# The norm roots' Newton steps and the exponentials' biases from VectorE to GpSimd, with a new order of work in the layers

## The chip, the cores and the metric

One core of a Trainium2 chip runs the whole program; the seven other cores are idle. The metric is the device time of one execution in microseconds (us). The kernel before takes 3483.93 us, the median of three runs (3475.66 to 3485.28).

## What is computed

Eight sequences ("images" below) of 512 tokens with 128 features go through a linear attention of Taylor features with a norm on either side, then through six layers, each of a local attention (16 heads of 64, windows of 32 tokens) and a gated feed-forward block, and through a last norm. All of it is float32. The change lies in the six layers:

```python
def attn_layer(x, Wqkv, qs, ksc, Wo):
    q, k, v = split(x @ Wqkv)               # 16 heads of 64
    q = l2norm(q) * qs
    k = l2norm(k) * ksc
    q = q * cos * scale + rotate_half(q) * sin * scale
    k = k * cos * inv + rotate_half(k) * sin * inv
    sim = q @ k2.T * 8                      # window and the one before it
    sim = where(mask, -big, sim)
    return (softmax(sim) @ v2) @ Wo

def ffn_layer(x, g, bln, W1, b1, W2, b2):
    xn = (x - mean(x)) / sqrt(var(x) + 1e-5) * g + bln
    a, gate = split(xn @ W1 + b1)
    return a * gelu(gate) @ W2 + b2

for i in range(6):
    x = attn_layer(shift_tokens(x), ...) + x
    x = ffn_layer(shift_tokens(x), ...) + x
```

## The kernel before

The program has no loop on the chip. `order()` lays every step of the whole run on one line by a time: a step of slot n stands at n plus its entry in the table `PLACE`. Each of the five engine programs walks this line and issues the instructions of its own steps in that order, with explicit waits on semaphores. So the table alone decides what is queued behind what, on each engine and on the DMA queue of SyncE (SP). An engine that waits holds up all that follows on it.

The layers have 48 units (one image in one layer). A unit has 8 slots of one head pair each and 4 rounds of two slots each; round m has the head pairs of slots 2m and 2m+1. The steps of one head pair lie many slots apart, so that a round mixes work of several pairs. The steps that matter here:

- `PJ` (TensorE): projection of Q and K of a head pair, three matmuls (`PS<-LXH,LH`, `PS<-LXL,LH`, `PS<-LXH,LL`) into one PSUM bank. `VP` is the same for V (`PS<-LH,LXH` and two more), `VC` its copy to `VV` on ScalarE.
- `PQ` (ScalarE, L1221): squares `SX`. `SS` (TensorE, `PS<-SX,C`): their sums over each head, 8 slots' halves to one PSUM tile.
- `PT` (VectorE, L938): the rotary products `TPB`, four per round; when it ends, the bank of its `PJ` is free. Projections, Wo and the feed-forward matmuls (`group`) share a ring of three banks, so that a `PJ` waits for the `PT` or copy that emptied the bank three groups earlier.
- `TS` (SP): swaps the halves of each pair through a DMA into `TR`. `AD` (GpSimd, L1350) adds them: final Q and K.
- `NM1`, `NM2`: norm roots for four slots at once, so twice in a unit. `NM1` takes the sums from PSUM (VectorE, L946) and does logarithm and exponential on ScalarE (L1024, L1026); `NM2` is one Newton step in three VectorE instructions on `NV` (L951, L953, L955, 128x128 each). `RW` (SP) writes the roots to DRAM, `RB` (SP, L518) reads them back as rows over 64 partitions, `PR` (GpSimd, L1332) multiplies K by them. `RQ` transposes them for the queries.
- `S1` (TensorE, mask `PS<-maskb,identb` and then `PS<-K,Q`): the scores of a round in banks 0 and 1. It waits for `PR` and for the exponentials of the round before, `S3`.
- `MX` (VectorE): the row maximum (L962), and then the exponential's bias `BQ`, minus the maximum times the query's root (L967, 128x16).
- `S3` (ScalarE, L1245): 16 exponentials with `BQ` as their bias, in four parts.
- `SU` (VectorE, L973, L975): sum and reciprocal. `NP` (GpSimd, L1358) scales by it. `TT` (VectorE, L981, L984): transposes. `PX`, `PY` (SP): move parts of them into `PP`.
- `PV` (TensorE, `PS<-PP,VV`): the product with V, in two halves (`PV` 0 and 1), and `PVn` (ScalarE) its copy.
- `WO` (TensorE, `PS<-AOT,LO`): Wo, once in a unit, and its addition to `X` on VectorE (L991, L992). Then the norm `F1`, `F2`, `F2n`, `F3` and the block `F4`, `F5`.

By what they hold besides the common steps, the four rounds of a unit are called here the plain round, the Wo round (`WO`, `NM1`, `NM2`), the norm round (`F1`, `F2`, `F2n`, `F3`) and the block round (`F4` and `F5` of that image, `NM1`, `NM2`).

Of the kernel before, what the change touches and what calls it, by code (L numbers as in the profile page):

```python
# [10 lines left out]
ALU = mybir.AluOpType  # L11
# [4 lines left out]
F1 = 341  # L16
# [10 lines left out]


PLACE = {
# [13 lines left out]
}  # L43

CONST = {}
# [261 lines left out]
def build(nc, xin, cst, awq, awk, awv, awo, wqkv, wo, w1, w2, vec, out):  # L307
    o = order()
    no = o.no
    with ExitStack() as ctx:  # L310
# [138 lines left out]
        def sync_program(e):  # L449
# [10 lines left out]
            for st, key in o.line:  # L460
# [40 lines left out]
                elif st == "RW":  # L501
                    q, = key
                    if q > 1:
                        for n in (4 * q - 6, 4 * q - 5):
                            on.wait_ge(f"rb_in{n % 2}", 32 * (n // 2) + 32)
                    on.wait_ge("nm_dve", 4 * q + 4)
                    for c in range(4):
                        e.dma_start(rootd[q % 2, :, 128 * c:128 * c + 128], NV[32 * c:32 * c + 16, 2, :]).then_inc(sem[f"rr_in{q % 2}"], 16)
                elif st == "RB":
# [29 lines left out]
        def tensor_program(e):  # L539
# [9 lines left out]
            for st, key in o.line:  # L549
# [135 lines left out]
                elif st == "SS":  # L685
                    i, = key
                    if i % 8 == 0 and i:
                        on.wait_ge("nm_dve", 4 * (i // 8) - 3)
                    on.wait_ge("pj_act", i + 1)
                    sel = cn("tsel")[:, 32 * (i % 8):32 * (i % 8) + 32]  # L690
                    for c in range(4):
# [35 lines left out]
                    p.then_inc(sem["s1_pe"], 1)  # L727
                elif st == "RQ":
                    q, = key
                    on.wait_ge("nm_dve", 4 * q + 4)  # L730
                    free(on, st, key)
                    e.transpose(bk(st, key)[:, 0:128], NV[:, 2, :], ident).then_inc(sem["rq_pe"], 1)
                elif st == "PV":
# [66 lines left out]
        def vector_program(e):  # L800
# [35 lines left out]
            for st, key in o.line:  # L836
# [104 lines left out]
                elif st == "NM1":  # L941
                    q, = key
                    if q:
                        on.wait_ge("nm_dve", 4 * q)
                    on.wait_ge("ss_pe", 8 * q + 8)
                    e.tensor_scalar(NV[:, 0, :], nb[:, 0:128], 1e-24, None, ALU.max).then_inc(sem["nm_dve"], 1)  # L946
                elif st == "NM2":
                    q, = key
                    v, u, x = NV[:, 0, :], NV[:, 1, :], NV[:, 2, :]
                    on.wait_ge("nm_act", 2 * q + 2)  # L950
                    e.tensor_tensor(u, v, x, ALU.mult).then_inc(sem["nm_dve"], 1)  # L951
                    on.wait_ge("nm_dve", 4 * q + 2)
                    e.scalar_tensor_tensor(u, u, -0.5, x, ALU.mult, ALU.mult).then_inc(sem["nm_dve"], 1)  # L953
                    on.wait_ge("nm_dve", 4 * q + 3)
                    e.scalar_tensor_tensor(x, u, 1.5, x, ALU.add, ALU.mult).then_inc(sem["nm_dve"], 1)  # L955
                elif st == "MX":
                    m, = key
                    g = PS[:, 0:2, :].rearrange("p s (g k) -> p (s g) k", k=64)
                    on.wait_ge("s1_pe", m + 1)
                    if m:  # L960
                        on.wait_ge("s1_dve", 2 * m)
                    e.tensor_reduce(MX[:, :], g, AX_X, ALU.max).then_inc(sem["s1_dve"], 1)  # L962
                    on.wait_ge("s1_dve", 2 * m + 1)
                    if m > 1:
                        on.wait_ge("s3_act", 4 * m - 4)
                    on.wait_ge("rq_act", m // 2 + 1)
                    e.scalar_tensor_tensor(BQ[m % 2][:, :], MX[:, :], -1.0, rq(m), ALU.mult, ALU.mult).then_inc(sem["s1_dve"], 1)  # L967
                elif st == "SU":
                    m, = key
                    if m > 1:  # L970
# [47 lines left out]
        def scalar_program(e):  # L1018
# [20 lines left out]
            for st, key in o.line:  # L1039
# [182 lines left out]
                elif st == "NM1":  # L1222
                    q, = key
                    if q:
                        on.wait_ge(f"rr_in{(q - 1) % 2}", 64 * ((q - 1) // 2) + 64)
                        on.wait_ge("rq_pe", q)
                    on.wait_ge("nm_dve", 4 * q + 1)
                    ln_exp(NV[:, 1, :], NV[:, 0, :], NV[:, 2, :], -0.5, "nm_act", q + 1)
                elif st == "VC":
                    j, = key  # L1230
# [5 lines left out]
                elif st == "S3":  # L1236
# [2 lines left out]
                    if m > 1:  # L1239
                        on.wait_ge("tt_dve", 2 * m - 2)  # L1240
                    on.wait_ge("rq_act", m // 2 + 1)
                    on.wait_ge("s1_dve", 2 * m + 2)
                    for g in range(4 * h, 4 * h + 4):
                        at = 64 * (g - 8 * s)
                        p = e.activation(SC[m % 2][:, g, :, :].rearrange("p x k -> p (x k)"), bank[s][:, at:at + 64], ACT.Exp,  # L1245
# [38 lines left out]
        def gpsimd_program(e):  # L1284
# [4 lines left out]
            for st, key in o.line:  # L1289
# [27 lines left out]
                elif st == "WL":  # L1317
# [6 lines left out]
                        hi, lo, src = LH[:, 256 * c:256 * c + 256], LL[:, 256 * c:256 * c + 256], WS[:, i % 3, :]  # L1324
                    on.wait_ge("wc_act", i + 1)
                    e.tensor_tensor(lo, src, hi.bitcast(F32), ALU.subtract).then_inc(sem["wc_pool"], 1)
                elif st == "PR":
                    n, = key
                    dst = K[:, n % 8, :]
                    on.wait_ge("ad_pool", 2 * n + 2)  # L1330
                    on.wait_ge(f"rb_in{n % 2}", 32 * (n // 2) + 32)
                    e.tensor_tensor(dst, dst, RB[n % 2][:, :], ALU.mult).then_inc(sem["pr_pool"], 1)  # L1332
                elif st == "XSl":
                    u, = key
                    b = u % NB
                    xh, xl = LX[u % 2]
                    on.wait_ge("xs_act", u + 1)
                    e.tensor_tensor(xl[:, :], X[:, b, 0:L], xh[:, :].bitcast(F32), ALU.subtract).then_inc(sem["xs_pool"], 1)
                elif st == "F3l":
                    u, = key  # L1340
                    on.wait_ge("xc_act", u + 1)
                    e.tensor_tensor(XCL[:, :], H[2][:, :], XCH[:, :].bitcast(F32), ALU.subtract).then_inc(sem["xc_pool"], 1)
                elif st == "AD":
                    i, = key
                    n, w = i // 2, i % 2
                    if n > 7:
                        on.wait_ge("s1_pe", n // 2 - 3)
                    on.wait_ge("pj_dve", i + 1)
                    on.wait_ge(f"t3_in{n % 2}", 32 * (n // 2) + 32)
                    e.tensor_tensor((Q, K)[w][:, n % 8, :], TPB[:, n % 3, w, :], TR[n % 2][:, w, :], ALU.add).then_inc(sem["ad_pool"], 1)  # L1350
                elif st == "NP":
                    m, = key
                    on.wait_ge("su_dve", 2 * m + 2)
                    if m == 0:
                        for z in PP:
                            e.memset(z[:, :, :, :], 0.0).then_inc(sem["zero_pool"], 1)
                    sc = SC[m % 2][:, :, :, :].rearrange("p g x k -> p g (x k)")
                    e.tensor_tensor(sc, sc, RC[m % 2][:, :].rearrange("p (g o) -> p g o", o=1).broadcast_to([128, 16, 64]),  # L1358
                                    ALU.mult).then_inc(sem["np_pool"], 1)
# [64 lines left out]
```

## Time and profile before

| what | value |
|---|---|
| median of three runs | 3483.93 us (3475.66 to 3485.28) |
| profiled execution, its own time | 3475.88 us |
| its span, first to last instruction | 3474.1 us |
| TensorE (PE) | 3179.2 us, 92% |
| weight loads (PEld), beside PE | 1975.5 us, 57% |
| VectorE (DVE) | 2763.6 us, 80% |
| ScalarE (ACT) | 2536.5 us, 73% |
| GpSimd (POOL) | 2044.8 us, 59% |

The profiled execution is one execution of the program. Its busy time of an engine is the time in which at least one of its instructions runs by the trace; the end of a matmul is modelled, so PE's share is an upper bound. Idle time is put down to what came last of all that the instruction waited for. The layers' first maximum starts at 580.1 us and the last at 3402.0 us, with 192 rounds; what is ahead is the linear attention, which the change leaves as it is.

### The profile page before, as it was taken

How to read it: one execution, taken by the hardware profiler on the slowest of the kernel's cores; microseconds unless marked ns; L12 is line 12 of the kernel's file. 1: busy time of each engine (PE TensorE's matmuls, PEld its weight loads, DVE VectorE, ACT ScalarE, POOL GpSimd, SP SyncE). 2: the span in 40 equal slices, each digit the busy share in tenths (PEclk: the TensorE clock that was granted, in tenths of full speed). 3: DMA queues.
4: the chain of work that ended last, by engine and by line, in shares of the span. 5: the costliest groups of instructions: out<-in, count | busy, mean ns of one | idle time of the engine just before them, and what ended most of it. 6: DMA issues, size and time to landing. Idle time of an engine off the chain costs nothing.

```text
span 3474.1 us, 125058 instructions
## 1 busy us (share of the span) xinstructions
PE 3179.2 (92%) x52744; PEld 1975.5 (57%) x52744; DVE 2763.6 (80%) x3420; ACT 2536.5 (73%) x5866; POOL 2044.8 (59%) x1559
## 2 busy tenths in 40 slices
PE   7999997899999999999999899999999999999986
PEld 3444434566666566656666566666666665655553
DVE  3656657888888888888888888888888888888883
ACT  4666664778777777768787878787777777787784
POOL 0000006767677666767677777677767676766661
PEclk9999998999999999999999999999999999999998
DMA  3223324444444444444444444444444444434431
GB/s 110 77 75 80 80 57 135 140 142 136 145 149 145 135 134 145 144 140 137 140 136 148 138 151 138 140 141 152 146 142 137 134 146 139 143 127 145 137 130 31
DMA packets 271821, 447.01 MB, mean 129 GB/s; under 512 B 84254, under 2 KB 122396, under 8 KB 271132
## 3 DMA queue, kind: packets, MB, share of 16 engines
q1 hardware_dynamic: 244944, 422.50, 37.3%
q10 hardware_dynamic: 26316, 16.52, 1.7%
q8 instruction: 415, 6.80, 0.8%
q14 instruction: 146, 1.20, 0.1%
HBM read 124.21 MB, written 7.34 MB: 38 GB/s over the span
## 4 chain that ended last, share of the span: by engine, by line
PE 47%; DVE 24%; ACT 13%; issue 7%; SPq 3%; DMA 2%; POOL 2%; DVEq 0%; ACTq 0%; POOLq 0%
PE PS L542 47%; DVE TPB L938 8%; ACT SC L1245 8%; DVE SM L973 2%; DVE MX L962 2%; ACT SX L1221 2%; DMA RB<-root_scratch 2%; DVE NV L953 2%; DVE NV L951 1%; DVE PP L981 1%; POOL K L1332 1%; DVE H L1006 1%; SPq L477 1%; DVE NV L955 1%; ACT H L1024 1%
## 5 line engine op out<-in xcount | busy, mean ns | idle before, releaser
L938 DVE SCALAR_TENSOR_TENSOR TPB<-PS,VEC,C 128x1024 f32<-128x1024 f32 x768 | 959.1, 1269 | 98.7 <-ACT SX L1221 91.2
L1245 ACT ACTIVATE SC<-PS,BQ,RQ 128x64 f32<-128x64 f32 x3072 | 977.7, 437 | 40.0 <-DVE BQ L967 39.8
L1221 ACT ACTIVATE SX<-PS 128x512 f32<-128x512 f32 x768 | 468.6, 638 | 355.0 <-PE PS L542 347.9
L1332 POOL TENSOR_TENSOR K<-K,RB 128x512 f32<-128x512 f32 x384 | 496.2, 1292 | 286.8 <-DMA RB<-root_scratch 273.4
L1358 POOL TENSOR_TENSOR SC<-SC,RC 128x1024 f32<-128x1024 f32 x192 | 366.1, 1907 | 409.3 <-DVE RC L975 409.3
L542 PE MATMUL PS<-LXH,LH 128*128 128x512 f32 x768 | 379.2, 494 | 153.3 <-DVE TPB L938 145.9
L1350 POOL TENSOR_TENSOR K<-TPB,TR 128x512 f32<-128x512 f32 x384 | 499.2, 1300 | 0.0
L1350 POOL TENSOR_TENSOR Q<-TPB,TR 128x512 f32<-128x512 f32 x384 | 497.6, 1296 | 0.0
L542 PEld LDWEIGHTS PS<-PP,VV 64*64 64x64 f32 x12288 | 279.8, 136 | 149.7 <-issue 146.2
L542 PE MATMUL PS<-PP,VV 64*64 64x96 f32 (+1 forms) x12288 | 352.6, 250 | 4.3 <-DMA PP<-PX 2.0
L542 PE MATMUL PS<-AOT,LO 128*128 128x512 f32 x768 | 342.4, 599 | 0.0
L973 DVE TENSOR_REDUCE SM<-SC 128x16 f32<-128x1024 f32 x192 | 234.0, 1219 | 125.3 <-ACT SC L1245 123.8
L542 PE MATMUL PS<-K,Q 64*32 64x64 f32 (+1 forms) x24576 | 307.8, 225 | 26.8 <-issue 15.0
L542 PEld LDWEIGHTS PS<-LXH,LH 128*128 128x128 f32 x768 | 145.5, 189 | 313.1 <-DVE TPB L938 183.9
L542 PEld LDWEIGHTS PS<-K,Q 64*32 64x32 f32 x24576 | 293.0, 106 | 49.1 <-issue 19.9
L542 PE MATMUL PS<-LXH,LL 128*128 128x512 f32 x768 | 307.3, 400 | 0.0
L542 PE MATMUL PS<-LXL,LH 128*128 128x512 f32 x768 | 306.1, 399 | 0.0
L1235 ACT COPY VV<-PS 128x512 f32<-128x512 f32 x384 | 239.1, 623 | 89.2 <-PE PS L542 86.2
L542 PE MATMUL PS<-SX,C 128*32 128x128 f32 x6144 | 254.8, 283 | 2.2 <-issue 1.3
L542 PEld LDWEIGHTS PS<-AOT,LO 128*128 128x128 f32 x768 | 142.0, 190 | 170.4 <-issue 170.2
L962 DVE TENSOR_REDUCE MX<-PS 128x16 f32<-128x1024 f32 x192 | 233.2, 1214 | 5.6 <-PE PS L542 5.1
L1298 POOL TENSOR_TENSOR XR<-XR,T 128x512 f32<-128x512 f32 x8 | 10.2, 1276 | 365.6 <-DVE T L908 365.6
(166 smaller groups left out, 5862.8 us busy)
## 6 DMA issues: line engine op xcount, KB each, us to landing
TR<-TPB SPq DMA_DIRECT2D x768, 256.0 KB, 2.7
RB<-root_scratch SPq DMA_DIRECT2D x768, 128.0 KB, 3.0
PP<-PX SPq DMA_DIRECT2D x576, 64.0 KB
PP<-PP SPq DMA_DIRECT2D x384, 64.0 KB, 2.4
WS<-in_wqkv ACTq DMA_DIRECT2D x72, 128.0 KB, 2.5
PP<-PX SPq DMA_DIRECT2D x192, 48.0 KB
QA<-TH SPq DMA_DIRECT2D x128, 64.0 KB, 2.1
QA<-TL SPq DMA_DIRECT2D x128, 64.0 KB, 2.1
```

The costliest lines, as they stand in the source:

```text
L477: e.dma_start((QA, KA)[n][c::4, g % 6, :].bitcast(F32), (TH, TL)[low][rows, n, half, :].bitcast(F32)).then_inc(sem[f"qk_in{g % 2}"], 16)
L542: return e.matmul(dst, lhsT, rhs, start=start, stop=stop, **kw)
L938: e.scalar_tensor_tensor(TPB[:, n % 3:4 + n % 2:3 + n % 2 - n % 3, w, :], g, VEC[:, l, 9 + w:10 + w], C[:, at:at + 1024].rearrange("p (o c ...
L953: e.scalar_tensor_tensor(u, u, -0.5, x, ALU.mult, ALU.mult).then_inc(sem["nm_dve"], 1)
L962: e.tensor_reduce(MX[:, :], g, AX_X, ALU.max).then_inc(sem["s1_dve"], 1)
L973: e.tensor_reduce(SM[:, :], SC[m % 2][:, :, :, :].rearrange("p g x k -> p g (x k)"), AX_X, ALU.add).then_inc(sem["su_dve"], 1)
L1221: e.activation(SX[i % 3][:, :], bk("PJ", key)[:, :], ACT.Square).then_inc(sem["pj_act"], 1)
L1235: e.copy(VV[:, c, 512 * hf:512 * hf + 512], bk("VP", key)[:, :]).then_inc(sem["vp_act"], 1)
L1245: p = e.activation(SC[m % 2][:, g, :, :].rearrange("p x k -> p (x k)"), bank[s][:, at:at + 64], ACT.Exp, bias=BQ[m % 2][:, g:g + 1], scale ...
L1332: e.tensor_tensor(dst, dst, RB[n % 2][:, :], ALU.mult).then_inc(sem["pr_pool"], 1)
L1350: e.tensor_tensor((Q, K)[w][:, n % 8, :], TPB[:, n % 3, w, :], TR[n % 2][:, w, :], ALU.add).then_inc(sem["ad_pool"], 1)
L1358: e.tensor_tensor(sc, sc, RC[m % 2][:, :].rearrange("p (g o) -> p g o", o=1).broadcast_to([128, 16, 64]), ALU.mult).then_inc(sem["np_pool" ...
```

## The change

The Newton step `NM2` goes from three VectorE instructions to four on GpSimd. `MX` stays on VectorE as a maximum that is written negated, and its product with the query's root goes to GpSimd. The semaphores are split accordingly (`nm_pool`, `bq_pool`). All entries of `PLACE` for the layers' steps are new; those of the linear attention are the same.

```diff
 PLACE = {
-    "LS": 221.000, "LB": -1.200, "LO": -0.800, "S1": -0.074, "MX": 0.116, "S3": (0.544, 0.762, 0.998, 1.143),
+    "LS": 221.000, "LB": -1.200, "LO": -0.800, "S1": -0.240, "MX": -0.000, "S3": (0.424, 0.992, 0.802, 0.799),
...
                 elif st == "RW":
-                    on.wait_ge("nm_dve", 4 * q + 4)
+                    on.wait_ge("nm_pool", 4 * q + 4)
...
                 elif st == "NM1":
                     q, = key
                     if q:
-                        on.wait_ge("nm_dve", 4 * q)
+                        on.wait_ge("nm_pool", 4 * q)
                     on.wait_ge("ss_pe", 8 * q + 8)
                     e.tensor_scalar(NV[:, 0, :], nb[:, 0:128], 1e-24, None, ALU.max).then_inc(sem["nm_dve"], 1)
-                elif st == "NM2":
-                    q, = key
-                    v, u, x = NV[:, 0, :], NV[:, 1, :], NV[:, 2, :]
-                    on.wait_ge("nm_act", 2 * q + 2)
-                    e.tensor_tensor(u, v, x, ALU.mult).then_inc(sem["nm_dve"], 1)
-                    on.wait_ge("nm_dve", 4 * q + 2)
-                    e.scalar_tensor_tensor(u, u, -0.5, x, ALU.mult, ALU.mult).then_inc(sem["nm_dve"], 1)
-                    on.wait_ge("nm_dve", 4 * q + 3)
-                    e.scalar_tensor_tensor(x, u, 1.5, x, ALU.add, ALU.mult).then_inc(sem["nm_dve"], 1)
                 elif st == "MX":
                     m, = key
                     g = PS[:, 0:2, :].rearrange("p s (g k) -> p (s g) k", k=64)
                     on.wait_ge("s1_pe", m + 1)
                     if m:
-                        on.wait_ge("s1_dve", 2 * m)
-                    e.tensor_reduce(MX[:, :], g, AX_X, ALU.max).then_inc(sem["s1_dve"], 1)
-                    on.wait_ge("s1_dve", 2 * m + 1)
-                    if m > 1:
-                        on.wait_ge("s3_act", 4 * m - 4)
-                    on.wait_ge("rq_act", m // 2 + 1)
-                    e.scalar_tensor_tensor(BQ[m % 2][:, :], MX[:, :], -1.0, rq(m), ALU.mult, ALU.mult).then_inc(sem["s1_dve"], 1)
+                        on.wait_ge("bq_pool", m)
+                    e.tensor_reduce(MX[:, :], g, AX_X, ALU.max, negate=True).then_inc(sem["s1_dve"], 1)
...
                 elif st == "S3":
...
-                    on.wait_ge("s1_dve", 2 * m + 2)
+                    on.wait_ge("bq_pool", m + 1)
...
+                elif st == "MX":
+                    m, = key
+                    on.wait_ge("s1_dve", m + 1)
+                    if m > 1:
+                        on.wait_ge("s3_act", 4 * m - 4)
+                    on.wait_ge("rq_act", m // 2 + 1)
+                    e.tensor_tensor(BQ[m % 2][:, :], MX[:, :], rq(m), ALU.mult).then_inc(sem["bq_pool"], 1)
+                elif st == "NM2":
+                    q, = key
+                    v, u, x = NV[:, 0, :], NV[:, 1, :], NV[:, 2, :]
+                    on.wait_ge("nm_act", 2 * q + 2)
+                    e.tensor_tensor(u, v, x, ALU.mult).then_inc(sem["nm_pool"], 1)
+                    on.wait_ge("nm_pool", 4 * q + 1)
+                    e.tensor_tensor(u, u, x, ALU.mult).then_inc(sem["nm_pool"], 1)
+                    on.wait_ge("nm_pool", 4 * q + 2)
+                    e.tensor_scalar(u, u, -0.5, 1.5, ALU.mult, ALU.add).then_inc(sem["nm_pool"], 1)
+                    on.wait_ge("nm_pool", 4 * q + 3)
+                    e.tensor_tensor(x, u, x, ALU.mult).then_inc(sem["nm_pool"], 1)
```

What this and the new table do to the queues is seen at three places. The first is the block round on VectorE, before (`L1006` is `F4`, `L962` and `L967` are `MX`, `L981` and `L984` are `TT`, `L946` is `NM1`, `L938` is `PT`, `L951` to `L955` are `NM2`) and after:

```order
L962 TENSOR_REDUCE MX<-PS 128x16
L967 SCALAR_TENSOR_TENSOR BQ<-MX,RQ 128x16
L1006 SCALAR_TENSOR_TENSOR H<-PS,BI,H 85x512
L981 STREAM_TRANSPOSE PP<-SC 128x512
L984 STREAM_TRANSPOSE PX<-SC 128x512
L946 TENSOR_SCALAR NV<-PS 128x128
L938 SCALAR_TENSOR_TENSOR TPB<-PS,VEC,C 128x2x512
L951 TENSOR_TENSOR NV<-NV 128x128
L953 SCALAR_TENSOR_TENSOR NV<-NV 128x128
L955 SCALAR_TENSOR_TENSOR NV<-NV 128x128
L938 SCALAR_TENSOR_TENSOR TPB<-PS,VEC,C 128x2x512
L1014 SCALAR_TENSOR_TENSOR X<-PS,VEC,X 64x512
```

After, the same round of VectorE:

```order
L952 TENSOR_REDUCE MX<-PS 128x16
L991 SCALAR_TENSOR_TENSOR H<-PS,BI,H 85x512
L945 TENSOR_SCALAR NV<-PS 128x128
L966 STREAM_TRANSPOSE PP<-SC 128x512
L969 STREAM_TRANSPOSE PX<-SC 128x512
L937 SCALAR_TENSOR_TENSOR TPB<-PS,VEC,C 128x2x512 x2
L999 SCALAR_TENSOR_TENSOR X<-PS,VEC,X 64x512
```

The two `PT` now stand side by side, and `NM1` (`L945`) stands ahead of the transposes. On GpSimd, from one `NP` to the one after it in the same round, before:

```order
L1358 TENSOR_TENSOR SC<-SC,RC 128x1024
L1332 TENSOR_TENSOR K<-K,RB 128x512
L1350 TENSOR_TENSOR Q<-TPB,TR 128x512
L1350 TENSOR_TENSOR K<-TPB,TR 128x512
L1332 TENSOR_TENSOR K<-K,RB 128x512
```

and after:

```order
L1361 TENSOR_TENSOR SC<-SC,RC 128x1024
L1335 TENSOR_TENSOR K<-K,RB 128x512
L1318 TENSOR_TENSOR BQ<-MX,RQ 128x16
L1353 TENSOR_TENSOR Q<-TPB,TR 128x512
L1353 TENSOR_TENSOR K<-TPB,TR 128x512
L1323 TENSOR_TENSOR NV<-NV 128x128
L1325 TENSOR_TENSOR NV<-NV 128x128
L1327 TENSOR_SCALAR NV<-NV 128x128
L1329 TENSOR_TENSOR NV<-NV 128x128
L1335 TENSOR_TENSOR K<-K,RB 128x512
```

`BQ` stands behind `NP` and a `PR` in every round, and `NM2` between the two `PR` of the block round and of the Wo round. The second place is TensorE in the Wo round, from the end of a `PJ` on, before:

```order
L542 MATMUL PS<-LXH,LL 128x512
L542 MATMUL PS<-PP,VV 64x96 x14
L542 MATMUL PS<-PP,VV 64x64 x2
L542 MATMUL PS<-SX,C 32x128 x8
L542 MATMUL PS<-AOT,LO 128x512 x8
L542 MATMUL PS<-LXH,LH 128x512
L542 MATMUL PS<-LXL,LH 128x512
```

and after:

```order
L541 MATMUL PS<-LXH,LL 128x512
L541 MATMUL PS<-SX,C 32x128 x8
L541 MATMUL PS<-LXH,LH 128x512
L541 MATMUL PS<-LXL,LH 128x512
L541 MATMUL PS<-LXH,LL 128x512
L541 MATMUL PS<-AOT,LO 128x512 x8
L541 MATMUL PS<-PP,VV 64x96 x14
L541 MATMUL PS<-PP,VV 64x64 x2
```

The first half of the product with V has gone from ahead of `SS` to behind the second `PJ` (in all four rounds), and here behind Wo, while that `PJ` now stands ahead of Wo. The third place is SP's queue around `RW` (`L508`) in the block round (`L500` is `TS`, `L518` is `RB`, `L534` is `PY`), before:

```order
L527 DMA PP<-PX 32x4x96
L508 DMA root_scratch<-NV 16x128 x4
L534 DMA PP<-PX 32x512 x2
L500 DMA TR<-TPB 64x1024 x2
L518 DMA RB<-root_scratch 64x512 x2
```

and after:

```order
L526 DMA PP<-PX 32x4x96
L507 DMA root_scratch<-NV 16x128 x4
L517 DMA RB<-root_scratch 64x512 x2
L499 DMA TR<-TPB 64x1024 x2
L533 DMA PP<-PX 32x512 x2
```

`RB` is now ahead of `TS` in every slot, and directly behind `RW` where the roots are new; `PY` has gone behind both.

## Rows read from the trace of the kernel before

**Rows 1.** The page: span, busy time by engine, the chain that ended last

```profile
span 3474.1 us, 125058 instructions
...
PE 3179.2 (92%) x52744; PEld 1975.5 (57%) x52744; DVE 2763.6 (80%) x3420; ACT 2536.5 (73%) x5866; POOL 2044.8 (59%) x1559
...
PE 47%; DVE 24%; ACT 13%; issue 7%; SPq 3%; DMA 2%; POOL 2%; DVEq 0%; ACTq 0%; POOLq 0%
```

**Rows 2.** Layers' stretch: us, busy us of PE, PEld, DVE, ACT, POOL; clock, DMA

```profile
1700.00:2300.00 600.00, 559.40 (x10782) 367.95 (x10780) 515.41 (x607) 463.10 (x1137) 422.57 (x321) 1.00 0.43 142
```

**Rows 3.** Waits over the whole span: total us, times, longest

```profile
POOL SC L1358 <- DVE RC L975: 409.3, 101, 9.6
...
POOL K L1332 <- DMA RB<-root_scratch: 273.4, 155, 5.8
...
PE PS L542 <- DVE TPB L938: 164.0, 172, 4.4
```

**Rows 4.** Groups of VectorE: what the change takes away, and one product beside it

```profile
L953 DVE SCALAR_TENSOR_TENSOR NV<-NV 128x128 f32<-128x128 f32 x96 | 104.0, 1083 | 3.3
L967 DVE SCALAR_TENSOR_TENSOR BQ<-MX,RQ 128x16 f32<-128x16 f32 x192 | 89.2, 465 | 6.6
L951 DVE TENSOR_TENSOR NV<-NV 128x128 f32<-128x128 f32 x96 | 79.3, 826 | 2.3 <-ACT NV L1026 2.3
...
L955 DVE SCALAR_TENSOR_TENSOR NV<-NV 128x128 f32<-128x128 f32 x96 | 71.9, 749 | 3.3
```

**Rows 5.** Spread of two of them: min, median, max in ns

```profile
L953 DVE SCALAR_TENSOR_TENSOR NV<-NV x96: 291/1241/1409, 562.0 to 3370.4; 128x128 f32<-128x128 f32 x96
...
L967 DVE SCALAR_TENSOR_TENSOR BQ<-MX,RQ x192: 174/268/1321, 581.3 to 3403.3; 128x16 f32<-128x16 f32 x192
```

**Rows 6.** Groups of GpSimd, by shape

```profile
L1332 POOL TENSOR_TENSOR K<-K,RB 128x512 f32<-128x512 f32 x384 | 496.2, 1292 | 286.8 <-DMA RB<-root_scratch 273.4 <-DVE TPB L938 12.5
...
L1326 POOL TENSOR_TENSOR LL<-WS,LH 128x256 fp32r<-128x256 f32 x72 | 54.1, 752 | 18.3 <-ACT LH L1095 18.3
L1308 POOL TENSOR_SCALAR WS<-WS,VEC 128x682 f32<-128x682 f32 x6 | 12.1, 2011 | 0.0
...
L1287 POOL MEMSET CS<- 128x1 f32 x2 | 0.1, 98 | 0.3 <-POOLq L1414 0.3
```

**Rows 7.** TensorE in time: norm round and block round

```profile
2039.08 0.50 PE L542 MATMUL PS<-LXH,LH 128*128 128x512 f32 x1 [1.45 <-DVE TPB L938]
...
2049.70 0.88 PE L542 MATMUL PS<-PP,VV 64*64 64x96 f32 x32
...
2056.65 0.50 PE L542 MATMUL PS<-LXH,LH 128*128 128x512 f32 x1 [1.35 <-DVE TPB L938]
```

**Rows 8.** VectorE in time, the same block round

```profile
2053.10 0.69 DVE L951 TENSOR_TENSOR NV<-NV 128x128 f32<-128x128 f32 x1
...
2055.11 0.29 DVE L955 SCALAR_TENSOR_TENSOR NV<-NV 128x128 f32<-128x128 f32 x1
2055.32 1.28 DVE L938 SCALAR_TENSOR_TENSOR TPB<-PS,VEC,C 128x1024 f32<-128x1024 f32 x1
```

**Rows 9.** TensorE and VectorE in time, the Wo round

```profile
2017.07 7.13 PE L542 MATMUL PS<-AOT,LO 128*128 128x512 f32 x16
...
2024.24 0.68 DVE L991 TENSOR_TENSOR X<-PS,X 64x512 f32<-64x512 f32 x1 [3.78 <-PE PS L542]
```

**Rows 10.** TensorE, VectorE, ScalarE and GpSimd in time, the plain round

```profile
2059.83 0.41 PE L542 MATMUL PS<-maskb,identb 64*32 64x512 bf16 x8
...
2069.38 0.41 PE L542 MATMUL PS<-maskb,identb 64*32 64x512 bf16 x8
...
2063.25 0.18 DVE L967 SCALAR_TENSOR_TENSOR BQ<-MX,RQ 128x16 f32<-128x16 f32 x1
...
2066.80 2.53 ACT L1245 ACTIVATE SC<-PS,BQ,RQ 128x64 f32<-128x64 f32 x8
...
2065.30 1.30 POOL L1332 TENSOR_TENSOR K<-K,RB 128x512 f32<-128x512 f32 x1 [2.12 <-DMA RB<-root_scratch]
```

More of the change, by code:

```diff
@@ L687, in tensor_program @@
                     if i % 8 == 0 and i:
-                        on.wait_ge("nm_dve", 4 * (i // 8) - 3)
+                        on.wait_ge("nm_dve", i // 8)
                     on.wait_ge("pj_act", i + 1)
@@ L729, in tensor_program @@
                     q, = key
-                    on.wait_ge("nm_dve", 4 * q + 4)
+                    on.wait_ge("nm_pool", 4 * q + 4)
                     free(on, st, key)
@@ L1226, in scalar_program @@
                         on.wait_ge("rq_pe", q)
-                    on.wait_ge("nm_dve", 4 * q + 1)
+                    on.wait_ge("nm_dve", q + 1)
                     ln_exp(NV[:, 1, :], NV[:, 0, :], NV[:, 2, :], -0.5, "nm_act", q + 1)
```

23 rows, old and new, of the table PLACE are left out of this document.

## Prediction

> **What bounds the kernel now.** I read the page first. TensorE is busy for 92% of the span and holds 47% of the chain that ended last, VectorE holds 24% of it [rows 1]. In a stretch of 600 us within the layers TensorE is busy for 559 us, VectorE for 515 us, ScalarE for 463 us and GpSimd for 423 us [rows 2]. So no engine is full. TensorE is nearest to it, and the question is what its gaps wait for. The waits name it: 164.0 us of TensorE's idle time, in 172 pieces, end with the rotary product `PT` on VectorE, which empties a projection's bank [rows 3]. That is the most that the matmul row could win from an earlier `PT` alone, unless later `PT` also hide in slower starts that count as busy.
>
> Then the trace in time, for where those pieces lie. In a unit two of them are plain: a `PJ` of the norm round waits 1.45 us, and one of the block round 1.35 us [rows 7]. Times 48 units these two make 70 + 65 = 135 of the 164 us. What is late ahead of the second is seen on VectorE: `PT` starts at 2055.32, and the three instructions of `NM2` stand in front of it from 2053.10 on [rows 8]. The length of a unit follows from the first and the last of the 192 row maxima at 580.1 and 3402.0 us: 4 x 2821.9 / 191 = 59.1 us.
>
> **What is removed from VectorE.** `NM2` takes 104.0 + 79.3 + 71.9 us and `BQ` 89.2 us, together 344.4 us [rows 4], or 7.2 us a unit of the 0.859 x 59.1 = 50.8 us that VectorE is busy [rows 2]. Most of this isn't arithmetic: the middle Newton instruction takes 291 ns at best and 1241 ns in the median, `BQ` 174 ns at best and 1321 at worst [rows 5]. In the stretches that I read, the long ones end with an instruction of GpSimd.
>
> *Block round.* Without `NM2` the second `PT` can start up to 2055.32 - 2053.10 = 2.2 us earlier [rows 8]; TensorE waited 1.35 us for it [rows 7]. The whole wait goes: 48 x 1.35 = **65 us**. Bounds: nothing, if another wait takes its place, and 48 x 2.2 = 106 us, if waits in other units are longer. I take the wait that the row shows.
>
> *Norm round.* Here the late `PT` stands behind the norm's own Newton step, which stays. Only `BQ` goes from ahead of it: 0.465 us in the mean [rows 4], 48 x 0.465 = **22 us**; bounds 48 x 0.174 = 8 and 48 x 1.32 = 63 us [rows 5], the latter still below the wait of 70 us.
>
> *Wo round.* Before, VectorE stands idle for 3.78 us until Wo's matmuls of 7.13 us are done [rows 9], then adds, then turns to a `PT`. After, a further `PJ` stands ahead of Wo, so that its `PT` (1.28 us, [rows 8]) and half of the exponentials lie beside Wo. `NM2` was in that shadow already and brings nothing. TensorE's matmuls behind Wo showed hardly a gap, so between 0 and 1.28 us I take 0.4: 48 x 0.4 = **19 us**; bounds 0 and 61.
>
> **What is added to GpSimd.** No 128x128 and no 128x16 instruction of GpSimd is in the trace. Below 512 columns there is one row: 752 ns for 256 against 1292 for 512 [rows 6], which makes 2.1 ns a column and 0.21 us at the start. By this line a product of 128 columns takes 0.48 us and `BQ` 0.24 us. The instruction with two constants runs at 2011 ns for 682 columns [rows 6], hence (2011 - 210) / 682 = 2.6 ns a column and 0.55 us. `NM2` is 3 x 0.48 + 0.55 = 2.0 us; bounds are four times 0.098 = 0.4 and four times 0.752 = 3.0 us, `BQ` between 0.098 and 0.752 [rows 6]. Over the run that is 96 x 2.0 + 192 x 0.24 = 238 us, 5.0 us a unit on top of 0.704 x 59.1 = 41.6 [rows 2]: GpSimd comes to 79% of the unit before. `NM2` lands where it has time: behind it GpSimd waits for `SU` before `NP`, 409.3 us in 101 pieces, so about 4 us in each of two rounds of a unit [rows 3]. This cover costs nothing. If it were gone, 2.0 us in two rounds would be 192 us.
>
> The Trainium skill (GPSIMD Engine Reference, section Engine selection) says to keep elementwise work on VectorE since GpSimd takes about twice as long with two inputs. By that rule the step is twice 4 x 0.29 = 2.3 us instead of 2.0, an estimate; the trace bears it out only where VectorE is free, since its mean of 1.08 us for one of these instructions is no shorter than that.
>
> **What is moved.** `NM1` stands ahead of `TT` and can make VectorE wait for `SS`. But `SS` comes earlier by one half of `PV`, 0.88 us [rows 7], and `NM1` by `TT`, of about the same size; I take 0. `RB` stands ahead of `TS`, and behind `RW` at once. That pulls in the wait for `RB`, 273.4 us in 155 pieces [rows 3], and pushes `TS` and then `AD`; the two go against each other, and I take 0 between -2.1 and +2.1 us in the plain round (the wait there, [rows 10]). The four parts of `S3` change places, and what waits for them waits for all four: nothing.
>
> **The new wait.** `S3` now waits for GpSimd's `BQ`, which stands behind `NP` and a `PR`. Where that hurts is the plain round. `BQ` ends at 2063.43, the last exponentials at 2069.33, and the next mask matmul starts at 2069.38: the loop scores, maximum, bias, exponentials, scores is tight, 9.55 us from mask to mask [rows 10]. Each us by which `BQ` is late there is a us of the kernel. Bounds: 0, if GpSimd stands ready, and 3.4 us, if it must wait for the roots like the `PR` at 2065.30, which ends at 2066.60, and then takes its 0.24 [rows 10]. With `RB` issued earlier I take half of a `PR` less what VectorE took, 0.5 us: 48 x 0.5 = **24 us** lost. In the other rounds Wo, the norm and the block lengthen the round on TensorE beyond this loop; cost 0.
>
> **Sum.** -65 - 22 - 19 + 24 = -82 us. Against the profiled execution's own 3475.9 us this makes 3394 us. The median of the three runs lies 8 us above that execution, so 3402; I say **3400 us**, 2.4% less than 3484.
>
> **Rivals.** (a) *The bias is caught in GpSimd's queue.* At 3.4 us in each plain round, 163 us are lost against 106 won: 3484 + 57 = 3541 us. It decides from 106 / 48 = 2.2 us of lateness on. For it: the `PR` of that round did wait for its roots [rows 10], and those wait for an `NM2` that is itself now behind two `AD`. Against: `RB` no longer stands behind `TS` and `PY`, and GpSimd's time in the block round is spare.
>
> (b) *Nothing moves.* TensorE is busy 93% of the layers [rows 2], and VectorE's freed time turns into idle time, because scores, exponentials and roots set the pace: 3484 us, give or take 10. For it: VectorE has 14% of idle time there already. The skill says something near it (Perfetto Trace Analysis, section Optimizing Scalar/DVE Operations): work put from VectorE to GpSimd might not help since they share an SBUF read port. Against: the rows of the block round, where the wait sits directly behind `NM2`.
>
> (c) *All of the wait goes.* The 164 us of `PT` waits go [rows 3] and the plain round doesn't lose: 3484 - 164 = 3320 us. For it: every `PT` has 7.2 us a unit less ahead of it. Against: the norm round keeps its own Newton step.
>
> **How the numbers follow.** Chances: 0.60 for the forecast (3355 to 3445: 82 us with the bounds of the three gains and the one loss partly taken), 0.17 for (c), 0.10 for (b), 0.13 for (a). A difference below 0.3% (10 us) is about what the three runs can't tell from none. Faster: 0.60 + 0.17 and a little of (b), 0.78. Same: 0.08. Slower: (a) and a hundredth of (b), 0.14. The range is 3315 to 3490 us: it reaches over (c) and (b) and leaves out (a).
>
> **What would show it.** In the profile after: the three `NV` lines gone from VectorE, its busy time down by about 340 us; GpSimd's up by about 240, with `NV` products near 0.48 us and `BQ` near 0.24; the TensorE wait for `TPB` down from 164 to below 90 us, with the piece in the block round gone and that in the norm round left at about 1 us; the wait for `SU` on GpSimd lower, that for `RB` lower; plain rounds of about 10 us from mask to mask. Wrong would be: exponentials that wait for `BQ` in total by more than 100 us outside the Wo round, `K` products that still wait 2 us or more for `RB` in the plain round, or plain rounds of 12 us.

## The result: no gain, 0.4% slower

| | before | after |
|---|---|---|
| median, 8 runs each | 3485.8 us | 3498.3 us |
| ratio, 95% interval | | 1.0036 (1.0020 to 1.0052) |
| span of the profiled execution | 3474.1 us | 3505.7 us |
| VectorE busy | 2763.6 us | 2490.2 us |
| GpSimd busy | 2044.8 us | 2264.9 us |

Forecast were 3400 us and a range of 3315 to 3490 us. GpSimd's busy time rose by 220 us, near the 238 that were costed. VectorE's fell by 273 us and not by the 344 us of the instructions that left it: two that stayed took 46 us more (below), and the rest of the difference was not followed up. The time didn't follow either. First the page of the changed kernel, its parts 1 and 4 (against [rows 1]):

```profile
span 3505.7 us, 125202 instructions
...
PE 3206.9 (91%) x52744; PEld 1988.4 (57%) x52744; DVE 2490.2 (71%) x2940; ACT 2543.9 (73%) x5866; POOL 2264.9 (65%) x2135
...
PE 60%; DVE 9%; ACT 8%; DMA 8%; SPq 6%; issue 6%; POOL 3%; ACTq 0%; POOLq 0%; DVEq 0%
```

VectorE's share of the last chain fell from 24% to 9%. TensorE's rose from 47% to 60%, and those of DMA and of SP's queue from 2% and 3% to 8% and 6%. That is a first hint: part of the chain went from VectorE to transfers. Next the waits of the changed kernel over the whole span (against [rows 3]; who waits, for whom, total us, times, longest):

```profile
POOL BQ L1318 <- DVE MX L952: 223.0, 116, 3.8
...
DVE PX L969 <- DMA PP<-PX: 135.0, 53, 5.2
...
POOL SC L1361 <- DVE RC L960: 122.3, 60, 6.4
...
POOL K L1335 <- DMA RB<-root_scratch: 96.9, 62, 4.4
...
PE PS L541 <- DVE TPB L937: 92.3, 69, 4.5
...
PE PS L541 <- DMA PP<-PX: 74.5, 42, 4.1
...
ACT SC L1230 <- POOL BQ L1318: 66.0, 64, 3.6
```

TensorE's wait for `PT` went from 164.0 to 92.3 us, close to the expected 90. But a wait that hardly existed before (2.0 us) is there: TensorE waits 74.5 us and VectorE 135.0 us for `PP<-PX`, the transfers of `PX` and `PY`. What it is shows where it is longest. SP's queue, TensorE and VectorE of the changed kernel in time, one plain round:

```profile
2008.88 1.70 SPq L507 DMA_DIRECT2D root_scratch<-NV  x4
2011.70 1.48 SPq L517 DMA_DIRECT2D RB<-root_scratch  x2
2013.28 1.19 SPq L499 DMA_DIRECT2D TR<-TPB  x2
2014.51 1.26 SPq L533 DMA_DIRECT2D PP<-PX  x2
...
2021.83 1.06 PE L541 MATMUL PS<-PP,VV 64*64 64x96 f32 x32 [4.10 <-DMA PP<-PX]
...
2021.81 0.71 DVE L969 STREAM_TRANSPOSE PX<-SC 128x512 f32<-128x512 f32 x1 [5.18 <-DMA PP<-PX]
```

`RW` (L507) is issued until 2010.58. `RB` can't be before the roots have landed, at 2011.70. `TS` follows, and `PY` (L533) comes last, at 2014.51. It is issued until 2015.77, and those who wait for it start at 2021.8: 6 us for two transfers of 64 KB each that stand behind two of 128 KB and two of 256 KB. Both who need `PY` stop: the first half of `PV`, and the transpose that writes `PX` anew.

The length of each kind of round tells where the time is. It is the mean distance of the starts of the mask matmuls of successive scores, 47 or 48 rounds of each kind, in us:

| kernel | block | plain | Wo | norm | sum |
|---|---|---|---|---|---|
| before | 18.2 | 10.3 | 18.3 | 12.3 | 59.1 |
| after | 16.2 | 12.8 | 17.7 | 12.9 | 59.6 |

The block round gained 2.0 us and the plain round gave back 2.5. These are rounds of one profiled execution each, which lies up to 25 us off its kernel's median (that of e10; 10 us for before, 9 for after).

### The profile page after: what moved, and what is told of

Read it like the earlier page. It is cut to its first block, busy times and chain, and to the rows that moved or that the text cites. A ratio compares the mean times of both kernels' runs of the same rounds, so it can differ in the third digit from the quotient of the medians.

```text
span 3505.7 us, 125202 instructions
## 1 busy us (share of the span) xinstructions
PE 3206.9 (91%) x52744; PEld 1988.4 (57%) x52744; DVE 2490.2 (71%) x2940; ACT 2543.9 (73%) x5866; POOL 2264.9 (65%) x2135
## 4 chain that ended last, share of the span: by engine, by line
PE 60%; DVE 9%; ACT 8%; DMA 8%; SPq 6%; issue 6%; POOL 3%; ACTq 0%; POOLq 0%; DVEq 0%
PE PS L541 59%; DMA PP<-PX 5%; DVE TPB L937 3%; ACT SC L1230 2%; DMA root_scratch<-NV 2%; DVE H L805 2%; SPq L517 1%; SPq L507 1%; SPq L499 1%; DVE H L803 1%; ACT H L1009 1%; SPq L533 1%; SPq L476 1%; ACT SX L1206 1%; ACT FX L1011 1%
## 5 line engine op out<-in xcount | busy, mean ns | idle before, releaser
L1230 ACT ACTIVATE SC<-PS,BQ,RQ 128x64 f32<-128x64 f32 x3072 | 951.2, 440 | 68.1 <-POOL BQ L1318 66.0
L1335 POOL TENSOR_TENSOR K<-K,RB 128x512 f32<-128x512 f32 x384 | 515.1, 1341 | 97.1 <-DMA RB<-root_scratch 96.9
L1353 POOL TENSOR_TENSOR Q<-TPB,TR 128x512 f32<-128x512 f32 x384 | 511.5, 1332 | 63.3 <-DMA TR<-TPB 62.2
L541 PE MATMUL PS<-LXH,LH 128*128 128x512 f32 x768 | 364.4, 474 | 101.4 <-DVE TPB L937 89.0
L1220 ACT COPY VV<-PS 128x512 f32<-128x512 f32 x384 | 230.2, 600 | 292.8 <-PE PS L541 292.2
L541 PE MATMUL PS<-PP,VV 64*64 64x96 f32 (+1 forms) x12288 | 359.5, 255 | 74.7 <-DMA PP<-PX 74.5
L541 PEld LDWEIGHTS PS<-K,Q 64*32 64x32 f32 x24576 | 294.9, 106 | 41.9 <-issue 29.4
L952 DVE TENSOR_REDUCE MX<-PS 128x16 f32<-128x1024 f32 x192 | 233.9, 1218 | 37.6 <-PE PS L541 37.1
```

The source lines that it names most:

```text
L541: return e.matmul(dst, lhsT, rhs, start=start, stop=stop, **kw)
L952: e.tensor_reduce(MX[:, :], g, AX_X, ALU.max, negate=True).then_inc(sem["s1_dve"], 1)
L1220: e.copy(VV[:, c, 512 * hf:512 * hf + 512], bk("VP", key)[:, :]).then_inc(sem["vp_act"], 1)
```

## Experiments

Each was timed against the kernel before on the same chip, and the ratio is to that. e5 to e8 ran on another chip than the rest, so that a difference between one of them and another kernel is taken from their ratios. "PY early" is e1's order.

| label | table | Newton | bias | ratio (95%) | median us |
|---|---|---|---|---|---|
| after | new | GpSimd | GpSimd | 1.0036 (1.0020 to 1.0052) | 3498.3 |
| e1 | new, PY early | GpSimd | GpSimd | 0.9939 (0.9923 to 0.9955) | 3457.1 |
| e2 | new, SP as before | GpSimd | GpSimd | 1.0102 (1.0084 to 1.0120) | 3515.0 |
| e3 | old | GpSimd | GpSimd | 1.0193 (1.0177 to 1.0209) | 3546.2 |
| e4 | new | VectorE | VectorE | 1.0051 (1.0033 to 1.0070) | 3497.4 |
| e5 | old | GpSimd | VectorE | 0.9918 (0.9905 to 0.9931) | 3453.1 |
| e6 | old | VectorE | GpSimd | 1.0330 (1.0316 to 1.0345) | 3598.5 |
| e7 | new, PY early | GpSimd | GpSimd, ahead | 0.9897 (0.9885 to 0.9910) | 3448.8 |
| e8 | new, PY early | GpSimd | VectorE | 0.9906 (0.9893 to 0.9918) | 3450.3 |
| e9 | e8, one RB in four behind TS | GpSimd | VectorE | 0.9853 (0.9829 to 0.9878) | 3430.3 |
| e10 | as e9 | GpSimd | GpSimd | 1.0195 (1.0168 to 1.0222) | 3550.0 |
| e11 | e9, F2n later | GpSimd | VectorE | 1.0022 (1.0008 to 1.0037) | 3488.9 |
| e12 | e2's | GpSimd | VectorE | 0.9848 (0.9828 to 0.9867) | 3428.5 |

### First four: the queue of SP, or the bias on GpSimd?

**e1**, `PY` alone moved, on SP only:

```diff
-    "PY": 3.121,
+    "PY": 2.750,
```

> The changed kernel with one entry of the table altered: PY from 3.121 to 2.750, so that on SP's queue PY stands directly behind RW and ahead of RB and TS; nothing else moves. Theory 1 (the queue of SP): in the block round PY now waits on SP for RW's write to land and behind RB and TS, its 64 KB land behind their 768 KB, and PV 0 and the second transpose of the plain round wait for it (74.5 us of TensorE's and 135.0 us of VectorE's idle time in the changed kernel). It expects both waits below 10 us, the plain round down from 12.8 us to 10.5 to 11, and 3498 - 48 x (1.5 to 2.3) = 3390 to 3425 us. Rival, theory 2 (the bias in GpSimd's queue): the plain round is long because S3 waits for BQ behind a PR; it expects another wait in the same place, a plain round still above 12 us, and 3485 to 3500 us.

Measured: 0.9939. Both waits for `PP<-PX` are gone, as theory 1 said, and from 1.0036 on this is 0.0097 x 3484 = 34 us. But the plain round only falls from 12.8 to 11.9 us, not to its 10.5 to 11, and 3457 us lies between the ranges of both theories. The waits show what took the place (e1, whole span):

```profile
PE PS L541 <- DVE TPB L937: 134.0, 97, 3.9
...
ACT SC L1230 <- POOL BQ L1318: 112.9, 81, 3.9
...
DVE TPB L937 <- DMA TR<-TPB: 91.8, 57, 3.6
```

`TS` is the next one held behind `RB`: the rotary product waits for it to free its buffer, and ScalarE waits longer for the bias.

**e2**, all four of SP's entries as before:

```diff
-    "PX": 2.136, "PY": 3.121, "TS": -7.004, "RB": -3.007,
+    "PX": 2.427, "PY": 2.800, "TS": -6.939, "RB": -2.631,
```

> The changed kernel with the entries of PX, PY, TS and RB as they were before the change, so that SP's queue has the order of before, on all other engines the order of the changed kernel stays. Theory 1 expects the PY waits gone as in e1, and the waits of PR for RB back at about 270 us (RB behind TS again): 3400 to 3450 us, a little above e1. Theory 2 expects BQ, which stands behind that PR, to come later still: 3510 to 3560 us.

Measured: 1.0102, 3515 us, in theory 2's range, with ScalarE's wait for `BQ` at 182.5 us and that of `PR` for `RB` back at 288.7 us. So neither theory alone holds.

**e3**, the code of after with the whole old `PLACE`, and **e4**, the code of before with the whole new `PLACE`:

> The Newton step and the bias on GpSimd as in the changed kernel, with the whole table of before. Theory 1 expects the block round's wait of 1.35 us for PT gone (65 us) and some of it lost on late biases: 3410 to 3460 us. Theory 2 expects the bias behind a PR that waits for RB (273 us in the kernel before) to lengthen every plain round by 2 to 3.4 us: 3500 to 3560 us.

> The new table with the Newton step and the bias still on VectorE, in the places that the table gives NM2 and MX. Theory 1 expects the PY wait of the changed kernel in full and none of the relief on VectorE: 3550 to 3610 us. Theory 2, by which the table is harmless and the move to GpSimd costs, expects 3450 to 3490 us.

Measured: 1.0193 and 1.0051. e3 is in theory 2's range, and 5 us from rival (a) of the prediction. e4, at 3497 us, is slower than before, as theory 1 said, but it lies 53 us below theory 1's range and only 7 above theory 2's. Its waits for `PP<-PX` are 57.5 us on TensorE and 97.8 on VectorE, three quarters of those in the changed kernel. Each half of the change costs on its own, 0.5% and 1.9%, and both together only 0.4%, so each hides part of the other's cost.

### Second four: which of the two moved steps?

**e5** and **e6** split the move under the old table. e5's edit of the code of after (e6 is the reverse):

```diff
                 elif st == "MX":   # vector_program
...
+                    on.wait_ge("s1_dve", m + 1)
+                    if m > 1:
+                        on.wait_ge("s3_act", 4 * m - 4)
+                    on.wait_ge("rq_act", m // 2 + 1)
+                    e.scalar_tensor_tensor(BQ[m % 2][:, :], MX[:, :], -1.0, rq(m), ALU.mult, ALU.mult).then_inc(sem["bq_dve"], 1)
```

> The table of before, the Newton step on GpSimd, the bias on VectorE as before. Theory A (the bias waits in GpSimd's queue behind a PR that waits for its roots): nearly all of the 68 us that the move with the old table cost are the bias's; this kernel keeps the relief of the block round and is at 3430 to 3475 us. Rival B (the Newton step itself comes late on GpSimd, behind two AD, and with it the roots' trip through DRAM): 3520 to 3550 us.

> The table of before, the bias on GpSimd, the Newton step on VectorE as before. Theory A: 3530 to 3570 us, with ScalarE waiting 150 us or more for BQ. Rival B: 3475 to 3495 us, as before.

Measured: 0.9918 and 1.0330. e5 is in theory A's range. e6 is on its side, with 174.0 us of waits for `BQ`, but at 3599 us it is 29 us above its range. The directions are clear: the Newton step's move brings 29 us, the bias's costs 115 us. The two don't add up to e3: with the Newton step on GpSimd already, the bias costs 96 us (e5 to e3). In e5 the block round is 16.9 us against 18.2, 1.3 less, the plain round unchanged at 10.4, the norm round 0.4 longer and the Wo round 0.2.

**e7** gives the bias an entry of its own, ahead of the `PR` that waits for new roots, and **e8** puts it back on VectorE; both keep e1's `PY`.

```diff
+            lay(n + P["MX"] - 0.1 * (m % 2), o.put, "BQ", m)
...
-                elif st == "MX":    # gpsimd_program
+                elif st == "BQ":
```

> e1 with the bias of the odd rounds (plain and norm) ahead of the PR that waits for the new roots, instead of behind it, still on GpSimd. Theory A: ScalarE's wait for BQ falls from 112.9 us to below 70, the plain round from 11.9 to about 11 us, 3405 to 3435 us. Rival B: the plain round is set by the roots' trip (NM1, NM2, RW, RB, PR, AD, PR, S1) and stays at 11.9 us: 3450 to 3465 us.

> e1 with the bias back on VectorE, directly behind the maximum; the Newton step stays on GpSimd. Theory A: as e7, less the 0.2 to 1.3 us that VectorE needs for it in every round: 3405 to 3440 us. Rival B: 3450 to 3475 us.

Measured: 0.9897 and 0.9906. ScalarE's wait for `BQ` fell to 67.5 us in e7, as theory A said, but the times, 3449 and 3450 us, are 14 and 10 us above theory A's ranges and within 1 us of the rival's. With `RB` ahead of `TS` the bias's place is worth some 0.004 (e1 against e7), 15 us. The plain round stays at 11.6 and 11.8 us, so something else holds it.

### Last four: the order of RB and TS

**e9**: of four `RB`, the one that reads newly written roots goes behind `TS` on SP.

```diff
-        lay(n + P["RB"], o.put, "RB", n)
+        lay(n + P["RB"] + 0.057 * (n % 4 == 0), o.put, "RB", n)
```

> e8 (new table, PY behind RW, bias on VectorE) with one RB in four, the one that reads newly written roots, behind TS instead of ahead of it: RB's entry is later by 0.057 for it. Theory C (what is left of the plain round's excess over 10.3 us is TS, held on SP's queue behind an RB that waits for RW's write to land, and with it AD and PT): the plain round falls from 11.8 to 10.4 us and the kernel to 3375 to 3410 us. Rival D (the roots' trip RW, RB, PR, AD, PR, S1 is the limit, whatever the order of TS; a block round that is 2 us shorter is paid for by a plain round that is longer by nearly as much): 3440 to 3465 us.

Measured: 0.9853, 18 us below e8. The plain round is at 10.5 us, as theory C said. The rival has a part too: the Wo round went from 17.5 to 18.4 us, where TensorE now waits 0.5 us for `PR`, so that the kernel stays 20 us above the expected range.

**e10** makes the same edit to e1, whose bias is on GpSimd:

> e1 (bias on GpSimd, behind a PR) with the same one RB in four behind TS. By theory A the bias stands behind a PR whose roots now land later, and the gain of e9 is lost on it: 3460 to 3500 us, 50 us or more above e9. If the bias's place doesn't matter, it is equal to e9.

Measured: 1.0195, 0.0342 x 3481 = 119 us above e9, and at 3550 us also 50 us above the expected range. Its plain round is 13.0 us against 10.5. The two kernels differ only in where the bias is. The trace of e10 shows it, VectorE, GpSimd, ScalarE and TensorE in time, one plain round:

```profile
2036.37 1.22 DVE L952 TENSOR_REDUCE MX<-PS 128x16 f32<-128x1024 f32 x1 [0.24 <-PE PS L541]
...
2041.85 1.27 POOL L1335 TENSOR_TENSOR K<-K,RB 128x512 f32<-128x512 f32 x1 [5.53 <-DMA RB<-root_scratch]
2043.08 0.22 POOL L1318 TENSOR_TENSOR BQ<-MX,RQ 128x16 f32<-128x16 f32 x1
...
2043.39 1.29 ACT L1230 ACTIVATE SC<-PS,BQ,RQ 128x64 f32<-128x64 f32 x4 [4.76 <-POOL BQ L1318]
...
2048.78 0.63 PE L541 MATMUL PS<-maskb,identb 64*32 64x512 bf16 x8 [0.66 <-ACT SC L1230]
```

The maximum is ready at 2037.59. GpSimd stands 5.53 us in front of a `PR` that waits for its roots, and the bias, 0.22 us of work, comes at 2043.08. ScalarE stands idle for 4.76 us ahead of the exponentials, and the next scores wait for them.

**e11**: in e9 the image norm's Newton step stands between the two `PT` of its round (`"F2n": 14.623` to `14.800`).

> e9 with the Newton step of the image's norm on VectorE (F2n) between the two PT of the norm round instead of ahead of both. The norm round's wait of a projection for PT, 1.5 us in the changed kernel and 1.45 in the kernel before, ends with the PT behind F2n; with one PT ahead of it the round should fall from 12.9 to about 12 us, 20 to 45 us below e9. If F2n sets the pace through the block that follows, no gain or a loss up to 20 us.

Measured: 1.0022, 59 us slower than e9, and outside both expectations. The norm round went from 12.8 to 14.1 us and the block round stayed. TensorE's largest wait is before the next matmuls that need a bank of `F2`: 114 us over the run, 2.4 us in each norm round, against 31 us in e9. Its wait for `PT` fell from 84 to 28 us. The one was traded for the other. Together they are only 27 us longer; the rest is in the section on the hardware below.

**e12**: e2 with the bias on VectorE.

> e2 (SP's queue in the order of before) with the bias on VectorE instead of GpSimd, the Newton step on GpSimd. Theory A: the 3515 us of e2 were the bias behind a PR that waits for its roots; with it gone 3400 to 3440 us. Rival D: 3480 us or more.

Measured: 0.9848, against 1.0102 of e2: 0.0254 x 3481 = 88 us for the bias alone. e12 and e9 can't be told apart. Both are 1.5% faster than the kernel before and 1.8% faster than the changed one. e12 is also 0.0070, 24 us, below e5, which has the old order everywhere: that much the new order outside SP's queue is worth. The new table with SP's old order and both steps on VectorE was not run, so what the Newton step's move still brings under the new table isn't shown.

| kernel | block | plain | Wo | norm | sum |
|---|---|---|---|---|---|
| e1 | 16.1 | 11.9 | 17.6 | 12.8 | 58.5 |
| e2 | 16.3 | 13.2 | 18.5 | 11.9 | 59.9 |
| e3 | 16.9 | 12.9 | 18.4 | 12.4 | 60.7 |
| e5 | 16.9 | 10.4 | 18.5 | 12.7 | 58.5 |
| e6 | 19.0 | 11.3 | 18.5 | 12.6 | 61.5 |
| e9 | 16.7 | 10.5 | 18.4 | 12.8 | 58.3 |
| e10 | 16.1 | 13.0 | 18.2 | 12.8 | 60.0 |
| e12 | 16.8 | 10.3 | 18.4 | 12.6 | 58.1 |

## Why the prediction was wrong

Forecast and measured length by rounds, in us over the 48 units:

| | block | plain | Wo | norm | sum |
|---|---|---|---|---|---|
| forecast | -65 | +24 | -19 | -22 | -82 |
| changed kernel | -98 | +121 | -29 | +29 | +23 |
| e9 | -75 | +9 | +2 | +26 | -38 |

The miss is the plain round, by 97 us, and the norm round, by 51.

**What bounds the kernel, and the relief of the block round: right.** TensorE's wait for `PT` in the block round went (1.62 us a round before, by the same count that gave the table; below 0.02 after). The round gained 2.0 us with the whole change and 1.3 us with the Newton step alone (e5), against 1.35 forecast, or 65 us. That e5 comes so near is in part luck: the row showed 1.35 us where the mean wait was 1.62, and 0.58 us of it is left in e5; the new table took the rest.

**The prices on GpSimd: right, a little high.** `NM2` and the bias in the changed kernel, groups of GpSimd (busy us, mean ns, idle before):

```profile
L1325 POOL TENSOR_TENSOR NV<-NV 128x128 f32<-128x128 f32 x96 | 44.8, 466 | 7.5
L1323 POOL TENSOR_TENSOR NV<-NV 128x128 f32<-128x128 f32 x96 | 44.4, 462 | 32.4 <-ACT NV L1011 32.1
L1329 POOL TENSOR_TENSOR NV<-NV 128x128 f32<-128x128 f32 x96 | 44.0, 458 | 8.0
L1318 POOL TENSOR_TENSOR BQ<-MX,RQ 128x16 f32<-128x16 f32 x192 | 42.6, 222 | 224.0 <-DVE MX L952 223.0 <-DMA TR<-TPB 0.8
L1327 POOL TENSOR_SCALAR NV<-NV 128x128 f32<-128x128 f32 x96 | 28.6, 298 | 8.4
```

The line through two widths gave 480 ns for 458 to 466, and 240 for 222. The instruction with two constants took 298 ns for a forecast 550, because the row behind that figure was misread: L1308 in [rows 6] multiplies by one column of `VEC` and isn't this form. The sum is 204 us against 238.

**The step that failed: "`RB` stands ahead of `TS`, and behind `RW` at once ... I take 0".** It weighed `RB` against `TS` and left out `PY`, though front and prediction both had its new place. On SP's queue an `RB` of new roots waits for a write to DRAM to land, and everything behind it waits too. This put `PY` behind `RB` and `TS`, and it landed 6 us after its issue. The term put at 0 cost 52 us: undoing it for `PY` is worth 34 us (e1) and for `TS` another 18 us (e8 to e9).

**The step tied to it: "With `RB` issued earlier I take half of a `PR` less what VectorE took, 0.5 us: ... 24 us lost."** In the order of the changed kernel this term was on the safe side: between e1 and e8 the bias costs 11 us, not 24 (its cost with `PY` still late was not measured). The mechanism was named, the loop scores, maximum, bias, exponentials, and so was its other end, rival (a) at 3541 us. What was missed is that this term and the one above are one choice. With `RB` ahead of `TS`, the bias is cheap but `PY` and `TS` are late. With `TS` first, the bias costs 88 us (e12 to e2) or 119 us (e9 to e10). I had taken the benefit of the early `RB` in one sentence and not its price in the other.

In the old table the bias costs 115 us (e6), so rival (a) had the mechanism right for the move by itself. That e3's 3546 us lie so near to its 3541 is luck: the plain rounds lost 124 us there and not 163, and the other three won 48 us and not 106.

**The signs that were named.** Of the three signs of being wrong only the last came, plain rounds above 12 us. The exponentials' wait for `BQ` was 66.0 us in all, below 100, and that of `K` for `RB` 1.75 us in the mean plain round, below 2 though near it. A long plain round doesn't tell the two causes apart. The waits for `PP<-PX` did, and no sign was named for them.

**The norm round's 22 us: not there.** The round went from 12.3 to 12.9 us, and TensorE's wait for `PT` in it from 1.39 to 1.47. VectorE is free earlier, but its chain starts with the scores, for which it now waits (5.1 us over the run before, 37.1 after), and the norm's own instructions take longer. Two groups of VectorE in the changed kernel, which took 812 and 1104 ns before:

```profile
L807 DVE SCALAR_TENSOR_TENSOR FX<-H,FX 128x512 f32<-128x512 f32 x48 | 75.0, 1563 | 1.7
...
L805 DVE SCALAR_TENSOR_TENSOR H<-H,FX 128x512 f32<-128x512 f32 x48 | 63.2, 1318 | 1.6
```

Together that is 0.97 us more in each norm round. The traces show what makes them long. Where GpSimd was at work when one of these two began, in 92 cases of the changed kernel, it ended 545 to 553 ns after GpSimd's instruction ended. Where GpSimd was idle all along (four cases) it took 692 ns. `L803`, one of whose two inputs is in PSUM, kept to 668 to 693 ns in all 46 cases of the layers that began beside a GpSimd instruction. The Trainium skill (SBUF — State Buffer, section SBUF: two separate sides) says that a VectorE instruction with two SBUF inputs and a GpSimd instruction that reads SBUF exclude each other for the whole of an instruction; the trace agrees. But the work moved to GpSimd isn't all of it: with the new table alone (e4) the two already take 980 and 1445 ns, since the table puts other GpSimd instructions beside them: GpSimd was at work when 38 of the 48 `L807` began, against 8 before. In e2 they are at 1295 and 905 ns and the norm round is at 11.9 us, 0.4 shorter than before, which is the forecast relief.

**The Wo round's 19 us: there, and given back.** It fell by 0.6 us in the changed kernel (29 us over the run), and by as much with the table alone (e4). In e9 and e12, where the roots come behind `TS`, it is back at 18.4, with TensorE waiting for `PR` 0.5 and 0.7 us in each.

**The sum.** From the changed kernel at 1.0036, `PY` (34 us), the bias (11) and `TS` (18) lead to e9 at 0.9853. The rest, between 3430 and the forecast 3400 us, is by the table above the norm round, 48 us off in e9, and the Wo round, 21 off, less what block and plain round are better than forecast. The differences between e1, e8 and e9 are small and go over two chips, so that 11 and 18 us hold to some 7 to 10 us.

## What to carry to other kernels

A wait in an in-order queue is priced by what stands behind it. When a step goes to an engine with much idle time, ask what ends that idle time: if it is a transfer, the step inherits its lateness, and here 0.2 us of work in each turn of a tight loop cost about 100 us over the run. The same holds for a DMA queue: here an issue that waits for a landing did best behind the short transfers that others need, and its consumer's queue was then the wrong place for anything urgent. Split a combined change early: here one part of it gave 29 us by itself, one cost 115, and the new order hid most of the loss by making a new one.

## What was not expected of the hardware

**A loaded queue.** Transfers of 64 KB (`PP<-PP`) land in 2.3 us in the median of those that the trace resolves. `PY`'s took 6 us behind 768 KB that were issued on the same queue in the 3 us before it. The DMA engines were busy for 0.96 of the last 4.3 us of it, against 0.43 in the stretch of [rows 2]. More `RB` and `TS` were issued behind `PY` in that time; what part these had isn't shown.

**The clock.** The profiles show two levels of TensorE's granted clock, 1.2 and 2.4 GHz; the mean below is the share of the full one. In the plain round shown above, after TensorE had waited 4.10 us for `PP<-PX`, the clock is at the lower level from 2022.4 to 2025.8. The same matmul in it and behind it:

```profile
2024.70 0.63 PE L541 MATMUL PS<-LXL,LH 128*128 128x512 f32 x1
...
2027.45 0.39 PE L541 MATMUL PS<-LXL,LH 128*128 128x512 f32 x1
```

All kernels have the same 52744 matmuls, so that more busy time of TensorE is slower matmuls (their ends are modelled). From the profiled executions:

| kernel | span | TensorE busy | TensorE idle | mean clock |
|---|---|---|---|---|
| before | 3474.1 | 3179.2 | 294.9 | 0.979 |
| after | 3505.7 | 3206.9 | 298.8 | 0.968 |
| e6 | 3589.1 | 3218.7 | 370.4 | 0.963 |
| e9 | 3439.7 | 3173.8 | 265.9 | 0.977 |
| e10 | 3523.4 | 3205.3 | 318.1 | 0.964 |
| e11 | 3496.4 | 3203.0 | 293.4 | 0.965 |
| e12 | 3427.5 | 3164.0 | 263.5 | 0.981 |
| e2 | 3519.5 | 3224.4 | 295.1 | 0.955 |

The changed kernel's idle time is nearly that of the kernel before: the waits that it lost and those that it gained cancel, and 28 of the 32 us that its span is longer are busy time. By a mean clock of 0.979 and 0.968 the lower level held for 146 and 224 us; at (0.63 - 0.39) / 0.63 of that lost, the difference is 30 us, an estimate. So the prices above are of a wait and of the clock together. Of the bias's, 60 of 92 us are busy time between e12 and e2, 31 of 84 between e9 and e10, and 40 of 115 between before and e6; of e11's loss against e9 it is 29 of 57 us. The time at the lower level grew in rounds with the longer waits or behind them: in the plain rounds 83 us in the changed kernel against 8 before, in the norm rounds 130 us in e11 against 14 in e9, in the Wo rounds, which follow the plain ones, 166 us in e2 against 28 in e12. No run holds the clock fixed, and idle time alone doesn't set it: e10 and e6 have more of it than e2 and a higher clock.
